# A histogram comparison whose constant operand moves from SBUF to a PSUM bank

## The chip, the cores and the metric

The kernel runs on one NeuronCore of a Trainium2 chip. The core has a matrix engine (PE, TensorE), a vector engine (DVE, VectorE), a scalar engine (ACT, ScalarE), a general engine (POOL, GpSimd) and a queue engine for transfers (SP, SyncE). They run at the same time and are held together by semaphores only. SBUF is the on-chip memory for operands, PSUM the smaller one into which PE writes its sums; DVE and ACT can read and write both. The metric is the time of one execution on the device in microseconds (us), lower is better.

## The reference, cut to what matters

The program is a chain: a convolution block with 32 paths, local attention, and a mixture-of-experts layer whose gate is a graph attention over 262,144 random edges between 16,384 nodes. The part that matters here prepares and runs the graph attention:

```
e      = leaky_relu(a_src[src] + a_dst[dst])
alpha  = softmax of e over the edges with one dst
agg    = segment_sum(h[src] * alpha, dst)        # scores of the experts
hh     = gelu(x @ W1[ei] + b1[ei]); out += g * (hh @ W2[ei] + b2[ei])
```

The kernel sorts the edges by dst in an earlier phase. To know where each node's edges end, it counts the edges of each node (a histogram over 16,384 nodes) and sums the counts up.

## The kernel before, in words

Seven phases follow one another, with a barrier of all engines between them. The change lies in the fifth, `edge_phase` (from L1333), which runs from about 2829 us to 5962 us of the profiled span. Each engine has its own hand-written instruction list there.

**Histogram.** Each dst is split into two digits of 7 bits. For one group of 8 edges per partition, DVE makes two comparison masks ("hot"), one per digit: it compares the constant row 0..127 (`iota`), repeated 8 times, with 8 digits, each repeated 128 times. That is one `tensor_tensor` of 128 partitions x 1024 elements per digit (L1491), f32 in and bf16 out. There are 256 groups, so 512 such instructions; PE multiplies the two masks of a group in 8 matmuls of 128x128 (L1614) that all add into `psC`, which is a part of the PSUM bank `psH[0]`. The masks have two buffers, so DVE is at most two groups ahead of PE. Then DVE turns the counts into positions (L1498 to L1509) and signals `placed`.

**Gathers.** POOL issues one indirect DMA for each of the 16 x 128 columns of edges (L1453): 128 rows of the table `scratch_table`, picked by the edge's src that lies in the SBUF tile `edge[s]`, into `row[s]`. There are AHEAD = 4 buffers, so the first 4 x 128 = 512 gathers wait for nothing but the edges. POOL's list is: `e_zeros` memset, 512 gathers, one gather of first values (L1460), then a wait for the constants, for the zeros in `scratch_b` and for `placed`, then 128 scatters (L1465) that place each node's value at the position of its first edge, a plain DMA (L1470), and then the other 1536 gathers in a loop, each group of 128 after a new load of `edge[s]`.

**Scans.** SP loads `bsrc` from `scratch_b` after all scatters have landed (L1422). DVE then runs the scans over the edges, chunk by chunk (L1529 to L1558), each after the 128 gathers of its chunk; ACT does the exponentials (L1590). SP stores the state and reloads `edge[s]`.

**Experts.** After `placed`, PE, ACT and DVE work through 49 tiles of the expert layer: PE multiplies into `psH[0]` to `psH[3]` (L1626), ACT applies Gelu (L1582), PE multiplies into `psY` (L1631), and DVE adds a bias that lies in SBUF to what it reads from `psY` (L1516). DVE's list takes 3 of these tiles before each scan chunk.

Nothing here is set by a planner; the order on each engine is the order of the code.

Of the kernel before, what the change touches and what calls it, by code (L numbers as in the profile page):

```python
# [12 lines left out]
ACT = mybir.ActivationFunctionType  # L13
# [110 lines left out]
HOT = 8  # L124
# [1208 lines left out]
def edge_phase(nc, io, z_dram, table_dram, adst_dram, digit_dram, edge_dram, node_dram, first_dram, b_dram, state_dram, y_dram):  # L1333
# [6 lines left out]
    with ExitStack() as ctx:  # L1340
        sb = lambda name, shape, dt=F32: ctx.enter_context(nc.sbuf_tensor(name, shape, dt))
        sb2 = lambda name, shape, dt=F32: [sb(f"{name}{i}", shape, dt) for i in range(2)]
        sem = lambda name: ctx.enter_context(nc.semaphore(name))
        sem2 = lambda name: [sem(f"{name}{i}") for i in range(2)]
# [5 lines left out]
        iota = sb("i_iota", [128, 128]); before = sb("i_before", [128, 128])  # L1350
        digit = [sb(f"i_digit{i}", [128, 2, FC]) for i in range(2)]
        hot = [[sb(f"i_hot{i}{d}", [128, HOT, 128], BF16) for d in range(2)] for i in range(2)]
# [18 lines left out]
        psH = [ctx.enter_context(nc.psum_tensor(f"f_psH{e}", [128, ZT], F32)) for e in range(EXPERTS)]  # L1371
        psY = [ctx.enter_context(nc.psum_tensor(f"f_psY{i}", [128, ZT // 128, EXPERTS * C], F32)) for i in range(2)]

        psC, psB = psH[0][:, 0:128], psH[1][:, 0:1]
        passed = sem("passed")
        const_in = sem("const_in"); weights_in = sem("weights_in"); zeroed = sem("zeroed"); b_zeroed = sem("b_zeroed"); b_placed = sem("b_placed")
        b_gathered = sem("b_gathered")
        b_in = sem2("b_in"); state_out = sem2("state_out")
        edge_in = [sem(f"edge_in{i}") for i in range(AHEAD)]; rows_in = [sem(f"rows_in{i}") for i in range(AHEAD)]
        hist_in = sem("hist_in"); zeroed_hot = sem("zeroed_hot"); digit_in = sem2("digit_in")  # L1380
        hot_ready = sem("hot_ready"); hot_used = sem("hot_used"); counted = sem("counted"); step = sem("step")
        totals = sem("totals"); based = sem("based"); placed = sem("placed"); placed_out = sem("placed_out")
        GROUPS = FC // HOT
# [13 lines left out]
        with nc.Block() as block:  # L1397
# [78 lines left out]
            def _(dve):  # L1476
# [5 lines left out]

                dve.memset(zero[:], 0.0).then_inc(zeroed_hot, 1)
                dve.wait_ge(hist_in, 32)
                with dve.Fori(0, NFC // 2) as turn:
                    for par in range(2):
                        dve.wait_ge(digit_in[par], (turn + 1) * 16)
                        for g in range(GROUPS):
                            dve.wait_ge(hot_used, turn * (2 * GROUPS) + par * GROUPS + g)
                            for d in range(2):  # L1490
                                m = dve.tensor_tensor(hot[g % 2][d][:], iota[:].unsqueeze(1).to_broadcast([128, HOT, 128]),  # L1491
                                                      digit[par][:, d, g * HOT:(g + 1) * HOT].unsqueeze(2).to_broadcast([128, HOT, 128]),
                                                      ALU.is_equal)
                            m.then_inc(hot_ready, 1)
# [73 lines left out]

            @block.scalar
            def _(act):  # L1570
                for a, name in ((w1, "ffn_w1"), (b1, "ffn_b1"), (w2, "ffn_w2")):
                    act.dma_start(a[:], io[name]).then_inc(weights_in, 16)
                for par in range(2):
                    act.dma_start(z[par][:], z_view[par]).then_inc(z_in[par], 16)
                act.wait_ge(weights_in, 48)

                def gelus(turn, q, load):

                    t, par = turn * (2 * PER) + q, q % 2
                    for e in range(EXPERTS):  # L1580
                        act.wait_ge(hid_ready, t * EXPERTS + e + 1)
                        act.activation(hid[e][:], psH[e][:], ACT.Gelu, bias=b1[:, e:e + 1]).then_inc(gelu_done, 1)  # L1582
                    if load:
                        act.dma_start(z[par][:], z_view[t + 2]).then_inc(z_in[par], 16)
                    act.wait_ge(y_done[par], turn * PER + q // 2 + 1)
                    act.dma_start(y_view[t], y[par][:]).then_inc(y_out[par], 16)

                def exps(turn, par):
                    act.wait_ge(limited, turn * 2 + par + 1)
                    act.activation(weight[:], drop[:], ACT.Exp).then_inc(exped, 1)  # L1590

                def both(turn, last):
                    for par in range(2):
                        for q in range(par * PER, (par + 1) * PER):
                            gelus(turn, q, not last or q < 2 * PER - 1)
                        exps(turn, par)

                with act.Fori(0, NFC // 2 - 1) as turn:
                    both(turn, False)
                both(NFC // 2 - 1, True)  # L1600
                gelus(NFC // 2, 0, False)
                act.wait_ge(y_out[0], 16 * (TILES_Z // 2 + 1))
                act.wait_ge(y_out[1], 16 * (TILES_Z // 2))
# [414 lines left out]
```

## Time and profile before

| | us |
|---|---|
| median of 3 runs | 6376.89 |
| lowest, highest | 6370.15, 6381.33 |
| profiled execution, its time | 6396.85 |
| profiled execution, its span | 6395.3 |

The span is what the profile covers; 1.55 us of the profiled execution's time lie around it. Busy shares over the whole span are POOL 50%, DVE 50%, PE 48% and ACT 20%, but they are means over phases with different limits: PE and DVE carry the convolution and the attention in the first 2600 us, while POOL is busy for nearly all of the rest. An indirect DMA on POOL shows as busy for as long as POOL works on issuing it; the transfer itself runs later on the DMA engines. In a list of instructions in order of time, "issue" ahead of an instruction is a gap in which the engine waited for nothing that the profile shows.

### The profile page before, as it was taken

Reading aid. Unit: us, or ns where it says so; the run is one execution under the profiler, and the core shown is the slowest. Engines: PE = TensorE matmul, PEld = TensorE weight load, DVE = VectorE, ACT = ScalarE, POOL = GpSimd, SP = SyncE. Lnnn points to the kernel's source line nnn. Section 1 sums busy time; section 2 is a strip of 40 time slices with the busy share of each in tenths; the row PEclk is TensorE's granted clock in tenths of the full one; section 3 lists DMA queues with packets and bytes.
Section 4 is the critical chain, followed back from the end, with each engine's and each line's share of the span. In section 5 each row is a group of like instructions: output and inputs, shape, how many; then the busy total and the mean of one; then the engine's idle time right before and its main releaser. Section 6 shows DMA issues by size and latency. Waiting matters only on the chain. (4 is left out here: it accounts for less than half of the span.)

```text
span 6395.3 us, 60586 instructions
## 1 busy us (share of the span) xinstructions
PE 3078.2 (48%) x16144; PEld 2121.2 (33%) x16144; DVE 3183.0 (50%) x4772; ACT 1270.0 (20%) x4613; POOL 3228.6 (50%) x3313
## 2 busy tenths in 40 slices
PE   2778777775998988454444004822222222222000
PEld 0334434333888887343333002511111111111000
DVE  4989888864877777349994002311110011111139
ACT  0112121112777776210000001200000000000000
POOL 0000000000665655138887776777777777777536
PEclk9788878775999999555555555555555555555555
DMA  6455555553655555330001101311111111111125
GB/s 143 78 84 87 83 83 83 82 79 67 92 88 83 89 84 78 98 87 8 8 9 20 8 4 50 88 31 33 22 27 33 33 33 33 32 32 29 26 74 212
DMA packets 584849, 385.76 MB, mean 60 GB/s; under 512 B 404800, under 2 KB 531552, under 8 KB 581744
## 3 DMA queue, kind: packets, MB, share of 16 engines
q1 hardware_dynamic: 385640, 221.54, 15.4%
q10 hardware_dynamic: 89320, 109.87, 9.4%
q0 software_dynamic: 109728, 52.69, 7.1%
q14 instruction: 120, 0.98, 0.1%
q8 instruction: 41, 0.67, 0.0%
HBM read 235.33 MB, written 147.68 MB: 60 GB/s over the span
## 5 line engine op out<-in xcount | busy, mean ns | idle before, releaser
L1453 POOL DMA_INDIRECT e_row<-scratch_table,e_edge x2048 | 2236.6, 1092 | 704.9 <-issue 674.7
L1631 PE MATMUL f_psY<-f_w,f_hid 128*128 128x64 f32 x1568 | 347.3, 423 | 1839.3 <-ACT f_hid L1582 1839.3
L1631 PEld LDWEIGHTS f_psY<-f_w,f_hid 128*128 128x128 f32 x1568 | 338.1, 332 | 1914.0 <-ACT f_hid L1582 1788.7
L925 POOL MEMSET a_wproj<- 128x128 f32 x1 | 0.2, 204 | 1544.2 <-POOLq L140 1544.2
L1533 DVE TENSOR_TENSOR e_e<-e_row,e_b 128x512 f32<-128x512 f32 x16 | 11.2, 698 | 1324.6 <-DMA e_row<-scratch_table,e_edge 1324.4
L768 DVE SCALAR_TENSOR_TENSOR acc<-psE,c_b,acc 128x448 f32<-128x448 f32 x840 | 568.0, 676 | 107.7 <-PE psE L461 91.2
L1491 DVE TENSOR_TENSOR i_hot<-i_iota,i_digit 128x1024 bf16<-128x1024 f32 x512 | 581.5, 1206 | 9.4 <-DMA i_before<-in_before 9.4
L461 PE MATMUL psE<-stack,c_w 72*128 72x448 bf16 x896 | 386.8, 450 | 335.6 <-DVE acc L768 181.5
L1030 ACT ACTIVATE prob<-psS,low 128x100 f32<-128x100 f32 x1568 | 512.3, 371 | 176.8 <-DVE low L1063 176.8
L448 PE MATMUL psH<-h,c_w 128*128 128x448 f32 x1008 | 525.5, 608 | 0.9 <-ACT h L551 0.9
L1614 PE MATMUL f_psH<-i_hot 128*128 128x128 bf16 x2048 | 264.7, 310 | 326.9 <-DVE i_hot L1491 326.9
L971 PE MATMUL psS<-keys,q_exp 84*128 84x100 f32 x3136 | 394.0, 283 | 53.3 <-DMA keys<-in_kfeat 53.0
L971 PEld LDWEIGHTS psS<-keys,q_exp 84*128 84x128 f32 x3136 | 378.4, 200 | 63.8 <-issue 58.7
L1590 ACT ACTIVATE e_weight<-e_drop 128x1024 f32<-128x1024 f32 x16 | 16.9, 1056 | 1851.9 <-DVE e_drop L1546 1851.9
L1030 ACT ACTIVATION_READ_ACCUMULATOR prob<-psS,low 128x1 f32 x1568 | 367.5, 234 | 0.0
L1626 PE MATMUL f_psH<-f_z,f_w 64*128 64x512 f32 x392 | 352.4, 1077 | 2.3 <-DVE i_posi L1509 2.3
L461 PEld LDWEIGHTS psE<-stack,c_w 72*128 72x128 bf16 x896 | 95.5, 111 | 709.9 <-DVE acc L768 479.0
L1614 PEld LDWEIGHTS f_psH<-i_hot 128*128 128x128 bf16 x2048 | 197.2, 141 | 394.3 <-DVE i_hot L1491 394.3
L945 POOL DMA_DIRECT2D scratch_t<-t x224 | 151.0, 678 | 333.2 <-issue 175.1
L1582 ACT ACTIVATE f_hid<-f_psH,f_b 128x512 f32<-128x512 f32 x196 | 129.4, 687 | 944.9 <-PE f_psH L1626 944.7
L933 POOL DMA_DIRECT2D val<-scratch_vpad x448 | 268.2, 601 | 68.7 <-PE psO L996 33.6
L1063 DVE TENSOR_REDUCE low<-psS 128x5 f32<-128x500 f32 x336 | 216.0, 643 | 149.8 <-PE psS L971 145.8
(273 smaller groups left out, 5401.0 us busy)
## 6 DMA issues: line engine op xcount, KB each, us to landing
stack<-scratch_parts ACTq DMA_DIRECT2D x504, 112.0 KB
e_row<-scratch_table,e_edge POOLq DMA_INDIRECT x2048
scratch_y<-f_y ACTq DMA_DIRECT2D x49, 512.0 KB
g_y<-scratch_y SPq DMA_DIRECT2D x28, 896.0 KB, 4.9
scratch_state<-e_state SPq DMA_DIRECT2D x16, 1536.0 KB, 6.0
val<-scratch_vpad SPq DMA_DIRECT2D x672, 35.0 KB
scratch_parts<-h2p ACTq DMA_DIRECT2D x56, 336.0 KB, 2.2
keys<-scratch_kpad SPq DMA_DIRECT2D x112, 155.0 KB
```

Of the source, the lines that this page charges most:

```text
L448: m = pe.matmul(psH2[:, 0:PIX].rearrange("p (y x) -> p y x", x=W), w2[:, tap, :], h1[:, ROWS * t + dy:ROWS * (t + 1) + dy, dx:dx + W], sta ...
L461: pe.matmul(psE[c % 2][:, 0:PIX], w3[:, c, :], stack[SLOT[t]][:, c, :], start=True, stop=True).then_inc(e_ready, 1)
L768: dve.scalar_tensor_tensor(acc[:, SLOT[t]], psE[c % 2][:, 0:PIX], b3[:, c:c + 1], acc[:, SLOT[t]], ALU.max, ALU.add).then_inc(stt_done, 1)
L933: pool.dma_start(val[st.par][ky * WIN:(ky + 1) * WIN], windows(n, s * QROWS + ky)).then_inc(v_rest[st.at], 16)
L971: m = pe.matmul(psS[bank][:, (blk - a) * KEYS:(blk - a + 1) * KEYS], q_exp[st.pair][:, par, blk].rearrange("k h m -> k (h m)"), keys[par][ ...
L1030: m = act.activation(prob[par][:, blk * KEYS:(blk + 1) * KEYS], psS[bank][:, (blk - a) * KEYS:(blk - a + 1) * KEYS], ACT.Exp, bias=low[par ...
L1063: dve.tensor_reduce(low[par][:, a:b], psS[bank][:, 0:(b - a) * KEYS].rearrange("p (b k) -> p b k", k=KEYS), AX.X, ALU.min)\
L1453: pool.indirect_dma_start(out=row[s][:, f, :], out_offset=None, in_=table_dram, in_offset=bass.IndirectOffsetOnAxis(ap=edge[s][:, 0, f:f + ...
L1491: m = dve.tensor_tensor(hot[g % 2][d][:], iota[:].unsqueeze(1).to_broadcast([128, HOT, 128]), digit[par][:, d, g * HOT:(g + 1) * HOT].unsq ...
L1614: m = pe.matmul(psC, hot[g % 2][1][:, c, :], hot[g % 2][0][:, c, :], start=False, stop=False)
L1626: pe.matmul(psH[e][:], w1[:, e, :], z[par][:], start=True, stop=True).then_inc(hid_ready, 1)
L1631: m = pe.matmul(psY[par][:, j, e * C:(e + 1) * C], hid[e][:, j * 128:(j + 1) * 128], w2[:, e, :], start=True, stop=True)
```

## The change

The kernel takes `psI`, 128 columns of the PSUM bank `psH[2]`, which nobody uses before the expert tiles. At the start of `edge_phase` ACT waits for the loads of `iota` and `before` (`hist_in`), copies `iota` from SBUF into `psI`, and signals `iota_set`; DVE waits for that once, ahead of its histogram loop. In the loop, the first operand of the 512 comparisons is `psI` where it was `iota`. The number of instructions, the shapes, the types and the other operand (`digit`, in SBUF) stay.

```
-        psC, psB = psH[0][:, 0:128], psH[1][:, 0:1]
+        psC, psB, psI = psH[0][:, 0:128], psH[1][:, 0:1], psH[2][:, 0:128]
...
-        hist_in = sem("hist_in"); zeroed_hot = sem("zeroed_hot"); digit_in = sem2("digit_in")
+        hist_in = sem("hist_in"); iota_set = sem("iota_set"); zeroed_hot = sem("zeroed_hot"); digit_in = sem2("digit_in")
...
                 dve.memset(zero[:], 0.0).then_inc(zeroed_hot, 1)
                 dve.wait_ge(hist_in, 32)
+                dve.wait_ge(iota_set, 1)
...
-                                m = dve.tensor_tensor(hot[g % 2][d][:], iota[:].unsqueeze(1).to_broadcast([128, HOT, 128]),
+                                m = dve.tensor_tensor(hot[g % 2][d][:], psI.unsqueeze(1).to_broadcast([128, HOT, 128]),
                                                       digit[par][:, d, g * HOT:(g + 1) * HOT].unsqueeze(2).to_broadcast([128, HOT, 128]),
                                                       ALU.is_equal)
...
             def _(act):
+                act.wait_ge(hist_in, 32)
+                act.activation(psI, iota[:], ACT.Copy).then_inc(iota_set, 1)
                 for a, name in ((w1, "ffn_w1"), (b1, "ffn_b1"), (w2, "ffn_w2")):
                     act.dma_start(a[:], io[name]).then_inc(weights_in, 16)
```

The only list that changes its sequence is ACT's, at the start of the phase. Before, behind the barrier (a row is an instruction's number, its line, its kind and tiles, and what it waits for; a semaphore may stand there under another name, since numbers are used again):

```order
490 L1221 UNCONDITIONAL_BRANCH
491 L1569 UNCONDITIONAL_BRANCH [waits barrier_Pool_Activation_PE_DVE_SP_release]
492 L1572 DMA f_w<-in_ffn_w 64x512
493 L1572 DMA f_b<-in_ffn_b 128x4
494 L1572 DMA f_w<-in_ffn_w 128x256
495 L1574 DMA f_z<-scratch_z 64x512 x2
496 L1598 UNCONDITIONAL_BRANCH [waits weights_in]
```

The same place with the change:

```order
490 L1221 UNCONDITIONAL_BRANCH
491 L1570 UNCONDITIONAL_BRANCH [waits barrier_Pool_Activation_PE_DVE_SP_release]
492 L1573 ACTIVATE f_psH<-i_iota 128x128 [waits hist_in]
493 L1575 DMA f_w<-in_ffn_w 64x512
494 L1575 DMA f_b<-in_ffn_b 128x4
495 L1575 DMA f_w<-in_ffn_w 128x256
496 L1577 DMA f_z<-scratch_z 64x512 x2
497 L1601 UNCONDITIONAL_BRANCH [waits weights_in]
```

The copy now stands ahead of the five loads of the expert layer, which are issued only after it. On DVE, PE, POOL and SP no instruction changes its place.

## Rows read from the trace of the kernel before

**Rows 1.** The page: spans in 40 slices (tenths busy), and POOL's costliest group.

```profile
PE   2778777775998988454444004822222222222000
...
DVE  4989888864877777349994002311110011111139
...
POOL 0000000000665655138887776777777777777536
...
L1453 POOL DMA_INDIRECT e_row<-scratch_table,e_edge x2048 | 2236.6, 1092 | 704.9 <-issue 674.7
```

**Rows 2.** POOL in time, start of the phase: start us, us, engine, line, [idle before].

```profile
2833.75 1.07 POOL L1453 DMA_INDIRECT e_row<-scratch_table,e_edge  x1 [4.12 <-issue]
...
2837.67 0.95 POOL L1453 DMA_INDIRECT e_row<-scratch_table,e_edge  x1 [0.30 <-issue]
...
2840.17 1.96 POOL L1453 DMA_INDIRECT e_row<-scratch_table,e_edge  x1 [0.30 <-issue]
```

**Rows 3.** POOL in time, end of the histogram and end of the first gathers.

```profile
3419.22 1.96 POOL L1453 DMA_INDIRECT e_row<-scratch_table,e_edge  x1 [0.30 <-issue]
3421.49 0.94 POOL L1453 DMA_INDIRECT e_row<-scratch_table,e_edge  x1 [0.31 <-issue]
...
3743.25 0.94 POOL L1460 DMA_INDIRECT e_b_first<-scratch_adst,e_first_ix  x1 [0.30 <-issue]
3744.50 1.03 POOL L1465 DMA_INDIRECT scratch_b<-e_node_dst,i_posi  x1 [0.30 <-issue]
```

**Rows 4.** L1453 alone in two stretches: us, POOL busy (count), clock, DMA share, GB/s.

```profile
2840.00:3421.00 581.00, 497.77 (x254) 0.50 0.08 14
3430.00:3740.00 310.00, 229.84 (x245) 0.50 0.12 15
```

**Rows 5.** DVE in time: the histogram's first merged row, and the last positions.

```profile
2838.91 61.44 DVE L1491 TENSOR_TENSOR i_hot<-i_iota,i_digit 128x1024 bf16<-128x1024 f32 x54 [9.43 <-DMA i_before<-in_before]
...
3424.86 0.30 DVE L1509 CAST i_posi<-i_pos 128x256 int32<-128x256 f32 x1
```

**Rows 6.** DVE's groups by shape: count, busy us, mean ns, idle before.

```profile
L1491 DVE TENSOR_TENSOR i_hot<-i_iota,i_digit 128x1024 bf16<-128x1024 f32 x512 | 581.5, 1206 | 9.4 <-DMA i_before<-in_before 9.4
...
L1073 DVE TENSOR_TENSOR prob<-prob,inv 128x1400 f32<-128x1400 f32 x112 | 181.1, 1617 | 3.9
...
L1085 DVE TENSOR_TENSOR own<-own 128x448 f32<-128x448 f32 x112 | 70.0, 625 | 3.9
...
L1516 DVE TENSOR_TENSOR f_y<-f_psY,f_b 128x1024 f32<-128x1024 f32 x49 | 59.6, 1216 | 417.8 <-PE f_psY L1631 417.8
...
L208 DVE COPY sort_key<-psTurn 128x512 f32<-128x512 f32 x28 | 28.2, 1009 | 1.4 <-PE psTurn L240 1.3
...
L1529 DVE TENSOR_TENSOR_SCAN e_b<-e_edge,e_b,e_bsrc 128x128 f32<-128x128 f32 x64 | 25.7, 465 | 448.4 <-DMA e_bsrc<-scratch_b 448.4
```

**Rows 7.** POOL and DVE in time, scan phase.

```profile
3963.44 1.22 DVE L1516 TENSOR_TENSOR f_y<-f_psY,f_b 128x1024 f32<-128x1024 f32 x1 [12.82 <-PE f_psY L1631]
3964.59 1.60 DVE L1529 TENSOR_TENSOR_SCAN e_b<-e_edge,e_b,e_bsrc 128x128 f32<-128x128 f32 x4
...
3974.16 2.26 DVE L1552 TENSOR_TENSOR e_part<-e_row,e_weight 128x2048 f32<-128x2048 f32 x1
...
3963.89 0.94 POOL L1453 DMA_INDIRECT e_row<-scratch_table,e_edge  x1 [0.30 <-issue]
...
3974.28 2.97 POOL L1453 DMA_INDIRECT e_row<-scratch_table,e_edge  x1 [0.30 <-issue]
...
3978.79 1.19 POOL L1453 DMA_INDIRECT e_row<-scratch_table,e_edge  x1 [0.30 <-issue]
```

**Rows 8.** DVE in time, convolution phase.

```profile
300.06 0.67 DVE L768 SCALAR_TENSOR_TENSOR acc<-psE,c_b,acc 128x448 f32<-128x448 f32 x1
300.66 1.21 DVE L202 TENSOR_TENSOR sort_key<-sort_other 128x1024 f32<-128x1024 f32 x1
301.79 0.67 DVE L768 SCALAR_TENSOR_TENSOR acc<-psE,c_b,acc 128x448 f32<-128x448 f32 x1
```

**Rows 9.** POOL in time: a pause, the scatters' end, the loop's first and last gather.

```profile
3892.65 0.98 POOL L1465 DMA_INDIRECT scratch_b<-e_node_dst,i_posi  x1 [2.96 <-issue]
...
3913.06 0.62 POOL L1470 DMA_DIRECT2D scratch_b<-e_b_first  x1 [1.41 <-DMA scratch_b<-e_node_dst,i_posi]
3943.86 0.99 POOL L1453 DMA_INDIRECT e_row<-scratch_table,e_edge  x1 [30.18 <-DMA e_edge<-scratch_edge]
...
5940.90 0.94 POOL L1453 DMA_INDIRECT e_row<-scratch_table,e_edge  x1 [0.30 <-issue]
```

**Rows 10.** DVE's group L1533; waits of PE and SP (us in total, times, longest).

```profile
L1533 DVE TENSOR_TENSOR e_e<-e_row,e_b 128x512 f32<-128x512 f32 x16 | 11.2, 698 | 1324.6 <-DMA e_row<-scratch_table,e_edge 1324.4
...
PE f_psH L1614 <- DVE i_hot L1491: 326.9, 256, 11.5
...
SPq L1418 <- DVE i_posi L1509: 76.8, 1, 76.8
```

**Rows 11.** ACT in time: its last small copy, the old position of the loads.

```profile
2826.33 0.29 ACT L1327 ACTIVATE t_rows<-t_psR 128x140 f32<-128x140 f32 x1 [3.27 <-PE t_psR L1309]
...
2829.10 0.56 ACTq L1572 DMA_DIRECT2D f_w<-in_ffn_w  x1
```

## What it does to the time: the prediction

> **What bounds the kernel now.** I read the page's slices first: from slice 27 on only POOL is busy, at 7 tenths or so, with PE at 2 and DVE at 0 to 1 [rows 1]. So the busy shares of the whole span say nothing of this phase; the question is who ends last in it. The waits answer: DVE waits 1324.6 us for the gathered rows in its 16 chunks [rows 10], and POOL's gathers wait for almost nothing but their own issue: 704.9 us over 2048 of them, 674.7 of it the usual gap [rows 1]. POOL's list is therefore the chain through the whole of the edge phase: 512 gathers, one more, 128 scatters, 1536 gathers.
>
> Then POOL in order of time. The first gathers take 0.95 us with a gap of 0.30 [rows 2]. From 2840.17 on they take 1.96, until 3419.22; the next, at 3421.49, takes 0.94 again [rows 2, 3]. Those two instants are the start and the end of DVE's 512 comparisons, which begin at 2838.91 [rows 5] and run without a gap (581.5 us busy in all [rows 6]). The two stretches by themselves: 254 gathers in the first with 497.77 us busy, mean 1.96; 245 in the second with 229.84, mean 0.94 [rows 4]. Something that DVE does in the histogram doubles the cost of a gather.
>
> What it is, the scan phase shows, where single DVE instructions meet gathers. A gather that starts at 3974.28, just inside a tensor_tensor with both inputs in SBUF (3974.16, 2.26 us long), takes 2.97 us: it ends 0.83 us after that instruction. A gather beside the scans, two SBUF inputs again but short ones, takes 1.19. But the gather at 3963.89 lies wholly inside an L1516 (3963.44, 1.22 us long), which adds an SBUF bias to a PSUM operand, and takes 0.94, as if alone [rows 7]. So a gather is held until the running DVE instruction ends if that has two SBUF inputs, and not if one of them is in PSUM. In the histogram the held gather plus its gap of 0.30 take 1.96 + 0.30 = 2.26 us, two DVE instructions (61.44 us for 54 in a merged row is 1.138 each [rows 5]).
>
> After the histogram POOL still has 252 gathers and the L1460 to go: DVE signals at 3425.2 [rows 5], POOL reaches the scatters at 3744.50 [rows 3]. For 319 us the positions lie ready. The histogram's own length is hidden; its effect on POOL is not.
>
> **The change part by part.**
>
> *The gathers.* The new comparison has the form of L1516: PSUM first, SBUF second, 128x1024. By rows 7 it holds no gather. Per gather the histogram stretch costs now: 3421.49 - 2840.17 = 581.32 us over 254 gathers = 2.289; the free stretch 3743.25 - 3421.49 = 321.76 us over 253 issues = 1.272 [rows 2 to 4]. Both contain the same kind of pauses, about 3 us once in 128 issues (one is visible at 3892.65 [rows 9]), two in each stretch, so they cancel. Gain: 254 x (2.289 - 1.272) = **258.3 us**. Bounds: below, if a gather stayed as slow as beside the scans, 1.19 + 0.30 = 1.49 in place of 1.25 [rows 7], the gain would be 258.3 - 254 x 0.24 = 197 us; above, nothing can make it faster than the free gather, 258 (a few us more if the unprofiled gather is shorter).
>
> The Trainium skill has two things on this (SBUF — State Buffer, section "Who interferes with whom"): a vector instruction with two SBUF inputs contends with a GpSimd instruction that reads SBUF, one with a single SBUF input does not. By that the sum is as above. But the same section argues, as an inference, that tensor_tensor does not stall a DMA's issue on GpSimd, because it takes only the read interface and writing descriptors needs the write interface; by that rule there would be no loss to take away and the time would stay at 6377. The trace disagrees with that inference: 1.96 against 0.94 us.
>
> *The comparison itself.* Reading PSUM may cost DVE more. Instruction to instruction, the SBUF comparison takes 1.13 to 1.14 us, and an element costs (1617 - 625) / (1400 - 448) = 1.042 ns by L1073 and L1085 [rows 6], 1.067 us for 1024; a sort comparison of the same size, both inputs in SBUF, starts its successor after 1.13 (300.66 to 301.79 [rows 8]). Beside it the L768, with PSUM in and 448 elements, starts its successor after 0.60 [rows 8]; 448/1024 of the element time is 0.467, so it has 0.13 us around its elements where the SBUF one has 0.065. That is +0.07 us an instruction. The nearest in shape, L1516, starts its successor after 1.15 (3963.44 to 3964.59 [rows 7]), +0.015; its mean length is 1216 against 1206 ns [rows 6]. So between 512 x 0.015 = 8 us and 512 x 0.07 = 36 us more histogram; I take 30, near the upper one, since the L768 rows stand among back-to-back work. A gain is excluded, the element rate being the same. The signal `placed` moves from 3425.2 to about 3456, at most 3461.
>
> The Trainium skill (Perfetto Trace Analysis, section "Optimizing Scalar/DVE Operations") gives about 60 ns of access overhead on SBUF and 125 ns on PSUM for DVE; by that it would be 512 x 0.065 = 33 us, and the rows of L768 agree with it (0.065 and 0.13).
>
> *What hides it.* POOL now reaches the scatters at 3744.5 - 258.3 = 3486.2. DVE's 3456 is 30 us earlier. The cover shrinks from 319 us to 30, but holds: it is gone when a comparison costs more than (3486.2 - 3425.2) / 512 = 0.12 us extra, a pitch above 1.255. From there on, each 0.01 us costs 5 us.
>
> *The copy on ACT.* One 128x128 activation, in the place of one like L1327 (0.29 us [rows 11]); DVE's start moves by 0.3 to 0.6 us, inside the cover, cost 0. Had it been on the chain, it would be that. Queued behind ACT's new wait are its five loads, so far issued from 2829.10 [rows 11], now from about 2839. Whoever needs them is PE, which waits for `placed` as well, 600 us later: cost 0. PE in the histogram waits 326.9 us for DVE [rows 10], so it has room at any rate. SP's store of positions (L1418) and the three expert tiles ahead of the first scan come 30 us later; DVE then idles 448.4 us before the first scan [rows 6], now about 448 - 258 - 30 = 160. Cost 0.
>
> *Behind it.* From L1465 on all is as before, shifted: scatters, L1470, SP's load, one chunk, `edge` reload, gather loop (3943.86 becomes 3686) [rows 9]. The loop stays POOL's; nothing in it reads the moved operand. No stall there goes, none comes.
>
> **Sum.** Span 6395.3 - 258.3 = 6137.0; the profiled time, 6396.85, becomes 6138.6. The median of the runs shown is 20 us below the profiled time (6376.89), so the prediction is 6376.89 - 258.3 = 6118.6, rounded **6119 us**, 4.05% less.
>
> **The rivals.**
>
> *A, the hold stays.* The second input may come through the contended path whatever the first is, or it is the bf16 output (L1516 writes f32) that holds. Then a gather still takes two comparisons. With comparisons 0.07 us longer and 254 gathers (two in each): +254 x 0.14 = +36 us, 6413, slower by 0.6%; with 0.015 longer +8, 6385. It decides as soon as the hold exists at all. For it: only a bf16 output differs from L1516. Against: the gather inside L1516 at 0.94, and L1552 with f32 output holding for 2.97 [rows 7], so the output's type is not what holds there. 5%.
>
> *B, half a hold.* Gathers at 1.49 as beside the scans: 6377 - 197 = 6180. For it: nothing with one SBUF input shows it. 3%.
>
> *C, DVE becomes the bound.* The repeated reads of the same 128 PSUM columns could be slow. From a pitch of 1.255 the gain shrinks: at 1.40 `placed` comes at 3425 + 512 x 0.263 = 3560, 74 us after POOL, and the time is 6193. It turns slower than before when the pitch passes 1.135 + 319/512 = 1.76 us. At the rate of the slowest DVE read of PSUM here, L208 with 1009 ns for 512 elements [rows 6], it would be 2.02 us, `placed` at 3425 + 453 = 3878, and the time 6377 + 134 = 6511. For it: L208. Against: L1516 has PSUM, a repeated operand and the same size at 1216 ns. 3% for the range between, 1% for slower.
>
> **How the numbers follow.** Forecast 88%, A 5%, B 3%, C 4%. The forecast's own range: the pauses may fall otherwise (3 us each, two of them), chance meetings of gathers and DVE in the loop of 1536 may differ by 10 us, the runs lie within 11 us of each other, and up to 6 us if DVE's pitch just passes 1.255: 6095 to 6145. B and C's near end are just outside; I set 6095 to 6150, which leaves out about 15%. A difference of 0.2%, 13 us, is what a measurement can tell from none. Faster: 0.88 + 0.03 + 0.03 = 0.94; same: A's low end, 0.02; slower: A's high end and C's far end, 0.04.
>
> **What would show each step.** The 254 gathers between 2840 and 3421 become some 460 in the same time, at 0.94 to 0.96 us; if they stay at 1.9 to 2.1, A holds; at 1.2, B. The group of L1492 shows the comparison's cost: 512 instructions in 590 to 617 us of busy time. L1460 stands near 3485 and the first scatter right behind it without a wait; a wait for DVE's `i_posi` there would be C. The last gather of the phase moves from 5940.90 [rows 9] by the same 258 us. The prediction is wrong if the gathers shorten and the end doesn't follow, which would need a chain that no row here shows.

## The result and the profile after

The changed kernel takes **6116.49 us** (median of 4 runs, 6115.78 to 6125.72) against 6373.52 us of the kernel before on the same chip (6369.09 to 6381.33): a ratio of 0.9594 [0.9575, 0.9613], 4.1% faster. The forecast was 6119. The profiled execution takes 6116.39 us, its span 6114.8.

First the page: slices, and the two groups that the change touches (the first answers to [rows 1], the second to [rows 6]).

```profile
DVE  4998888985587778536999214111111111100139
...
POOL 0000000000466556325777757777777777777536
...
L1453 POOL DMA_INDIRECT e_row<-scratch_table,e_edge x2048 | 1975.1, 964 | 704.1 <-issue 673.8
...
L1492 DVE TENSOR_TENSOR i_hot<-f_psH,i_digit 128x1024 bf16<-128x1024 f32 x512 | 579.3, 1208 | 7.6 <-ACT f_psH L1573 7.6
```

The gathers' busy time falls from 2236.6 to 1975.1 us and their idle time stays: 261.5 us less, where the medians differ by 257.0. While DVE is at 9, POOL now shows 7 tenths, as in the scan phase, where it showed 8 before, part of it time in which gathers were held. The comparison has not become dearer at all, 1208 ns against 1206.

POOL in order of time, from the phase's start to the end of the scatters, the loop's first gather, and one of its last (answers to [rows 2, 3, 9]).

```profile
2809.98 0.53 POOL L1446 MEMSET e_zeros<- 128x512 f32 x1 [8.38 <-POOLq L1221]
2813.89 1.07 POOL L1453 DMA_INDIRECT e_row<-scratch_table,e_edge  x1 [3.38 <-issue]
...
2822.80 0.94 POOL L1453 DMA_INDIRECT e_row<-scratch_table,e_edge  x1 [0.30 <-issue]
...
3464.85 0.94 POOL L1460 DMA_INDIRECT e_b_first<-scratch_adst,e_first_ix  x1 [0.30 <-issue]
3466.10 1.03 POOL L1465 DMA_INDIRECT scratch_b<-e_node_dst,i_posi  x1 [0.30 <-issue]
...
3634.67 0.62 POOL L1470 DMA_DIRECT2D scratch_b<-e_b_first  x1 [1.42 <-DMA scratch_b<-e_node_dst,i_posi]
3665.56 0.99 POOL L1453 DMA_INDIRECT e_row<-scratch_table,e_edge  x1 [30.27 <-DMA e_edge<-scratch_edge]
...
5659.54 0.94 POOL L1453 DMA_INDIRECT e_row<-scratch_table,e_edge  x1 [0.30 <-issue]
```

From the first gather to L1460 it is 3464.85 - 2813.89 = 650.96 us; before it was 3743.25 - 2833.75 = 909.50 [rows 2, 3]. The difference is 258.5 us. The scatters follow without a wait, and the stretch from L1460 to the loop's first gather is 200.7 us as before (3943.86 less 3743.25 is 200.6). The last gather moves by 281 us, not by 258, because in this execution the whole phase begins earlier (the first gather at 2813.89 instead of 2833.75, 19.9 us), and the loop of 1536 gathers is 3 us shorter (1994.0 against 1997.0). The 19.9 us belong to earlier stages that the change does not touch: the profiled execution of before lay 20 us above its median. The medians differ by 257.0.

L1453 alone in two stretches, during the histogram and after it (answers to [rows 4]; us, POOL busy and count, clock, DMA share, GB/s).

```profile
2820.00:3399.00 579.00, 430.94 (x458) 0.50 0.13 18
3405.00:3455.00 50.00, 35.53 (x39) 0.50 0.20 48
```

458 gathers in the histogram where 254 were, at a mean of 0.94 us in place of 1.96, the same as once DVE is done.

DVE's first merged row and its last positions (answers to [rows 5]).

```profile
2817.99 12.53 DVE L1492 TENSOR_TENSOR i_hot<-f_psH,i_digit 128x1024 bf16<-128x1024 f32 x11 [7.63 <-ACT f_psH L1573]
...
3401.77 0.29 DVE L1510 CAST i_posi<-i_pos 128x256 int32<-128x256 f32 x1
```

Instruction to instruction that is (12.53 - 1.21) / 10 = 1.132 us; the SBUF form, by the same working, had (61.44 - 1.21) / 53 = 1.136. The positions are ready at 3402, 63 us before POOL reaches L1460.

ACT in order of time: its copy, and the loads behind it (answers to [rows 11]).

```profile
2817.32 0.28 ACT L1573 ACTIVATE f_psH<-i_iota 128x128 f32<-128x128 f32 x1 [9.74 <-DMA i_before<-in_before]
2817.32 0.56 ACTq L1575 DMA_DIRECT2D f_w<-in_ffn_w  x1
```

The waits: in total, times, longest (answers to [rows 6, 10]).

```profile
DVE e_e L1534 <- DMA e_row<-scratch_table,e_edge: 1321.1, 12, 119.7
...
PE f_psH L1617 <- DVE i_hot L1492: 322.9, 256, 9.7
DVE e_b L1530 <- DMA e_bsrc<-scratch_b: 193.2, 1, 193.2
```

DVE's waits for rows are unchanged: the loop of 1536 gathers is still POOL's. Only the idle time ahead of the first scan shrinks, from 448.4 to 193.2 us.

### The profile page after: what moved, and what is told of

It is laid out like the page before. It is cut to its first block and busy times, and to the rows that moved or that the text cites. A ratio compares the mean times of both kernels' runs of the same rounds, so it can differ in the third digit from the quotient of the medians.

```text
span 6114.8 us, 60588 instructions
## 1 busy us (share of the span) xinstructions
PE 3076.0 (50%) x16144; PEld 2113.0 (35%) x16144; DVE 3180.6 (52%) x4772; ACT 1269.8 (21%) x4614; POOL 2967.1 (49%) x3313
## 5 line engine op out<-in xcount | busy, mean ns | idle before, releaser
L1453 POOL DMA_INDIRECT e_row<-scratch_table,e_edge x2048 | 1975.1, 964 | 704.1 <-issue 673.8
L1534 DVE TENSOR_TENSOR e_e<-e_row,e_b 128x512 f32<-128x512 f32 x16 | 11.2, 699 | 1321.4 <-DMA e_row<-scratch_table,e_edge 1321.1
L768 DVE SCALAR_TENSOR_TENSOR acc<-psE,c_b,acc 128x448 f32<-128x448 f32 x840 | 568.6, 677 | 110.8 <-PE psE L461 94.6
L1492 DVE TENSOR_TENSOR i_hot<-f_psH,i_digit 128x1024 bf16<-128x1024 f32 x512 | 579.3, 1208 | 7.6 <-ACT f_psH L1573 7.6
L933 POOL DMA_DIRECT2D val<-scratch_vpad x448 | 268.3, 601 | 68.7 <-PE psO L996 34.9
## 6 DMA issues: line engine op xcount, KB each, us to landing
stack<-scratch_parts ACTq DMA_DIRECT2D x504, 112.0 KB
```

The source lines that it names most:

```text
L768: dve.scalar_tensor_tensor(acc[:, SLOT[t]], psE[c % 2][:, 0:PIX], b3[:, c:c + 1], acc[:, SLOT[t]], ALU.max, ALU.add).then_inc(stt_done, 1)
L933: pool.dma_start(val[st.par][ky * WIN:(ky + 1) * WIN], windows(n, s * QROWS + ky)).then_inc(v_rest[st.at], 16)
L1453: pool.indirect_dma_start(out=row[s][:, f, :], out_offset=None, in_=table_dram, in_offset=bass.IndirectOffsetOnAxis(ap=edge[s][:, 0, f:f + ...
L1492: m = dve.tensor_tensor(hot[g % 2][d][:], psI.unsqueeze(1).to_broadcast([128, HOT, 128]), digit[par][:, d, g * HOT:(g + 1) * HOT].unsqueez ...
```

## The experiments

Twelve kernels were run, later and on five chips. On all five the kernel before takes 6829 to 6840 us (medians), not 6374, and each ratio below is against its runs on the same chip. Which chip the comparison above ran on is not known, so the 460 us may lie in the chip or in its condition at the time ("condition" below means this difference, whatever its cause); they turned out to matter for the change itself. None of the 460 us lies ahead of the edge phase: its first gather starts at 2813 us in e1, at 2814 in the changed kernel of the comparison.

**The theory** was that a gather is held to the end of the DVE instruction that runs when it starts, if both inputs of that instruction are in SBUF. The rivals were that something else in the change gives the gain (the order of ACT's loads), that the hold is a share of the time rather than an instruction, and that the place of the operand decides.

### e1: all of the change but the operand

```diff
-    m = dve.tensor_tensor(hot[g % 2][d][:], psI.unsqueeze(1)...
+    m = dve.tensor_tensor(hot[g % 2][d][:], iota[:].unsqueeze(1)...
```

> ACT still fills the PSUM columns and DVE still waits for it once, but the 512 comparisons read iota from SBUF as before. Theory (the gain is that a gather is not held by a comparison with two SBUF inputs): nothing is gained, 6373 us within 10, gathers in the histogram at 1.96 us. Rival (the gain comes from the start of the phase: ACT's five loads now stand behind the copy): a time near 6116.

Measured: 6832.85 us, ratio 1.0006 [0.9991, 1.0020]. The copy, the wait and the later loads are worth nothing. POOL of this kernel:

```profile
3000.99 1.98 POOL L1453 DMA_INDIRECT e_row<-scratch_table,e_edge  x1 [0.30 <-issue]
```

A gather in the histogram takes 1.96 us again, and from the first gather to L1460 it is 3728.20 - 2812.91 = 915.3 us.

### e2: SBUF for the first digit, PSUM for the second

```diff
+    m = dve.tensor_tensor(hot[g % 2][d][:], (iota[:], psI)[d].unsqueeze(1)...
```

> Only the second comparison of each pair reads PSUM; the first has both inputs in SBUF again. Theory, a held gather is let go when the running comparison ends: it then takes 0.83 to 0.9 us, the gap is 0.30, so the next gather wants the inputs some 1.2 us later, just after the PSUM comparison of 1.13 us, and meets the next SBUF comparison. It stays in step, one gather in 2.26 us, and the whole gain is lost: 6373 us within 12. Rival, the loss goes with the share of comparisons that hold: half of it, 6116 + 129 = 6245.

Measured: 6826.12 us, ratio 0.9989 [0.9975, 1.0003]. Half of the comparisons no longer hold, and nothing is gained. DVE and then POOL of this kernel, in order of time:

```profile
3000.26 1.21 DVE L1492 TENSOR_TENSOR i_hot<-i_iota,i_digit 128x1024 bf16<-128x1024 f32 x1
3001.39 1.21 DVE L1492 TENSOR_TENSOR i_hot<-f_psH,i_digit 128x1024 bf16<-128x1024 f32 x1
3002.52 1.21 DVE L1492 TENSOR_TENSOR i_hot<-i_iota,i_digit 128x1024 bf16<-128x1024 f32 x1
```

```profile
3000.33 1.97 POOL L1453 DMA_INDIRECT e_row<-scratch_table,e_edge  x1 [0.30 <-issue]
3002.60 1.95 POOL L1453 DMA_INDIRECT e_row<-scratch_table,e_edge  x1 [0.30 <-issue]
```

Each gather starts 0.07 to 0.08 us after an SBUF comparison has begun, is held for the rest of it, ends 0.83 us after it (3002.30 against 3001.47) beside the PSUM one, and after the gap of 0.30 meets the next SBUF one. A held gather with its gap and two comparisons are equally long, 2.27 us, and lock together. The same 0.82 to 0.83 us stand between the comparison's end and the gather's in 253 gathers of the histogram of before. So the hold goes by the instruction; a share of the time would have given half the gain.

### e3: SBUF and PSUM by turns, two comparisons each

```diff
+    m = dve.tensor_tensor(hot[g % 2][d][:], (iota[:], psI)[g % 2].unsqueeze(1)...
```

> Both comparisons of every second group of 8 edges have two SBUF inputs, the other groups read PSUM. The same number of holding comparisons as with one in each pair. Theory: a gather let go at the end of the first SBUF comparison misses the second (it is not asking for anything until 1.2 us later), so the next two run free and the one after is held: 3 gathers in two groups, 4.53 us, 1.51 each, 384 in the histogram in place of 464. Loss 80 x 1.25 = 100 us: 6216 within 15. Rival by share: 6245. Rival that any such comparison in the stretch keeps all gathers in step: 6373.

Measured: 6661.42 us, ratio 0.9735 [0.9705, 0.9765]; one run of the four, left out of the ratio, took 7124.19, as long as e4 below. Why is not known. DVE, then POOL:

```profile
3006.63 2.34 DVE L1492 TENSOR_TENSOR i_hot<-i_iota,i_digit 128x1024 bf16<-128x1024 f32 x2
3008.90 2.34 DVE L1492 TENSOR_TENSOR i_hot<-f_psH,i_digit 128x1024 bf16<-128x1024 f32 x2
3011.16 2.34 DVE L1492 TENSOR_TENSOR i_hot<-i_iota,i_digit 128x1024 bf16<-128x1024 f32 x2
```

```profile
3006.93 1.74 POOL L1453 DMA_INDIRECT e_row<-scratch_table,e_edge  x1 [0.30 <-issue]
3008.97 0.94 POOL L1453 DMA_INDIRECT e_row<-scratch_table,e_edge  x1 [0.30 <-issue]
3010.22 0.94 POOL L1453 DMA_INDIRECT e_row<-scratch_table,e_edge  x1 [0.30 <-issue]
```

Three gathers in 4.53 us, one of them held. The one at 3006.93 ends at 3008.67, 0.83 after its first comparison is over (3006.63 + 1.21 = 3007.84), although the second SBUF one is running by then: of the comparisons only the one that it meets at its start holds it. From the first gather to L1460 it is 3576.91 - 2826.12 = 750.8 us, 164.5 less than in e1. The lock theory gave 158, a share of the time 129.

### e4: the operands exchanged

```diff
-    psI.unsqueeze(1)..., digit[par][:, d, ...]..., ALU.is_equal)
+    digit[par][:, d, ...]..., psI.unsqueeze(1)..., ALU.is_equal)
```

> The digits in SBUF are the first operand and the PSUM columns the second. Theory (the number of SBUF inputs decides): 6116 us within 5, gathers 0.94. Rival (it is the place of the operand: the first operand from SBUF is what holds, or the second from PSUM costs more): gathers at 1.96 and 6373.

Measured: 7123.34 us, ratio 1.0429 [1.0405, 1.0454]: slower by 4.3%, which neither theory had. The gathers were not held, 0.94 to 0.95 us up to about 3050 us, so the operand's place does not decide the hold. From there on many take 1.09 us, 17 of them 1.79, most with no comparison running: the mean of the 512 is 1.02. And DVE stood still for 637.9 us in the histogram. Was that the exchange, or where it ran?

### e9: the changed kernel itself, once more

No edit.

> The changed kernel itself, once more. On the two chips of the experiments so far the kernel before takes 6829 and 6840 us where it took 6374 on the chip of the comparison, and kernels that differ from the changed one only in an operand's place or in 24 gathers take 7123 and 7141. Theory (what differs is the chip or its host, where the other engines are slowed while POOL issues gathers at full rate): if the kernel before takes some 6830 here too, the changed one takes about 7120 to 7140, 4% more, with DVE idle for 20 us at a time in the histogram; if the kernel before takes some 6374, it takes 6116. Rival (it is the swapped operands or the moved gathers that cost): 6116/6374 of the kernel before, 4% less, on any chip.

Measured: 7135.42 us, ratio **1.0433 [1.0410, 1.0455]**. It is not the exchange. The same program that was 4.1% faster in the comparison is 4.3% slower here. DVE in order of time: as the stall builds up, in it, and where it ends.

```profile
2814.18 5.74 DVE L1492 TENSOR_TENSOR i_hot<-f_psH,i_digit 128x1024 bf16<-128x1024 f32 x5
2824.98 2.36 DVE L1492 TENSOR_TENSOR i_hot<-f_psH,i_digit 128x1024 bf16<-128x1024 f32 x2 [5.05 <-remote]
...
2864.22 2.36 DVE L1492 TENSOR_TENSOR i_hot<-f_psH,i_digit 128x1024 bf16<-128x1024 f32 x2 [20.04 <-remote]
...
2998.62 2.36 DVE L1492 TENSOR_TENSOR i_hot<-f_psH,i_digit 128x1024 bf16<-128x1024 f32 x2 [20.04 <-remote]
3021.02 2.36 DVE L1492 TENSOR_TENSOR i_hot<-f_psH,i_digit 128x1024 bf16<-128x1024 f32 x2 [20.04 <-remote]
...
3527.15 73.62 DVE L1492 TENSOR_TENSOR i_hot<-f_psH,i_digit 128x1024 bf16<-128x1024 f32 x65 [12.34 <-remote]
```

And POOL, at the first gathers' end and after it:

```profile
3500.45 0.94 POOL L1460 DMA_INDIRECT e_b_first<-scratch_adst,e_first_ix  x1 [0.30 <-issue]
...
4032.99 1.03 POOL L1465 DMA_INDIRECT scratch_b<-e_node_dst,i_posi  x1 [531.60 <-DVE i_posi L1510]
```

While gathers run free, a group of two comparisons comes once in 22.40 us instead of once in 2.27. The stall builds up over the first groups and ends right after POOL's last gather (L1460 at 3500.45), from where DVE runs unbroken. So only 34 of the 256 groups are done when POOL is finished, and the rest follow at full pace: POOL waits 531.6 us for the positions. The stretch from the first gather to L1460 is 3500.45 - 2808.95 = 691.5 us, 223.8 less than in e1 and 40.5 more than in the comparison. So the change still gains 223.8 us on the gathers and loses 531.6 to the wait, 308 us on balance, beside 302.6 between the medians of e9 and e1. This is rival C of the prediction, DVE as the bound, by a cause that it did not name.

A group has 8 matmuls with 8 weight loads on PE, and 22.40 / 16 = 1.40. In the scan phase DVE waits for PE's expert tiles, of 40 matmuls and 40 weight loads each. In the comparison two of them follow each other in 13.4 to 14.2 us where nothing else stands between; in e9, while POOL issues gathers, in 112.2, and 80 x 1.40 = 112.0:

```profile
4420.30 1.22 DVE L1517 TENSOR_TENSOR f_y<-f_psY,f_b 128x1024 f32<-128x1024 f32 x1 [89.89 <-issue]
4532.46 1.22 DVE L1517 TENSOR_TENSOR f_y<-f_psY,f_b 128x1024 f32<-128x1024 f32 x1 [110.93 <-DMA scratch_vpad<-v]
```

On DVE itself the last 3 of the 16 scans of one chunk stand at the same interval, where nothing is waited for (two of them here); the 13 before them took 5.05 us together:

```profile
4723.95 0.54 DVE L1559 TENSOR_TENSOR_SCAN e_state<-e_weight,e_state,e_part 128x128 f32<-128x128 f32 x1 [1.53 <-issue]
4725.35 0.54 DVE L1559 TENSOR_TENSOR_SCAN e_state<-e_weight,e_state,e_part 128x128 f32<-128x128 f32 x1 [0.87 <-issue]
```

**The second theory**: in this condition, while POOL issues gathers once in 1.25 us, each other engine gets one instruction through in 1.40 us. That also fits the 460 us by which the kernel *before* is slower here. In e1, which takes as long, POOL waits 300.2 us in 6 places for the reload of `edge`, in the comparison 30 us in one place: 270 us. Another 168 lie behind the last gather (6829.7 - 6207.6 = 622.1 us to the end of the span, 454.4 before), since DVE, held up by the expert tiles, ends its scans 187 us after that gather in e1 and some 18 in the comparison.

One thing speaks against taking "one instruction in 1.40 us" word for word. PE in the stall:

```profile
3001.04 1.03 PE L1617 MATMUL f_psH<-i_hot 128*128 128x128 bf16 x8 [21.37 <-DVE i_hot L1492]
```

The 8 matmuls of a group stand 0.11 us apart, right behind DVE's signal, and end by 3002.07 (matmul ends are modelled), yet DVE goes on at 3021.02. So 1.40 is what the total comes to for each of PE's instructions; what passes in the 19 us between is not in the trace.

### e11: eight more matmuls of zeros in each group

```diff
+    pe.matmul(psC, zero[:], zero[:], start=False, stop=False)
```

> The changed kernel with 8 more matmuls in each group on PE (zeros times zeros, added to the same sum). On the slowed chips a group of 8 edges takes 22.40 us while gathers run free, with 2, 3 and 8 DVE instructions in a group alike. Theory (each instruction of PE, 8 weight loads and 8 matmuls in a group, costs 1.40 us there): 32 of them, a group in 44.8 us. Rival (the period comes from the signals between the engines, one pair a group): 22.4 us still. On a chip that is not slowed: 2.27 us, PE's 16 matmuls hidden behind DVE, and 6116.

Measured: 7180.85 us (one run). DVE:

```profile
3002.13 2.35 DVE L1492 TENSOR_TENSOR i_hot<-f_psH,i_digit 128x1024 bf16<-128x1024 f32 x2 [42.45 <-remote]
3046.93 2.35 DVE L1492 TENSOR_TENSOR i_hot<-f_psH,i_digit 128x1024 bf16<-128x1024 f32 x2 [42.45 <-remote]
```

The interval doubles to 44.80 us = 32 x 1.40 when PE's instructions in a group double and DVE's and the signals stay. So it goes by the number of PE's instructions, and the rival is refuted; how each comes to cost 1.40 us is not shown.

### e5, e6, e7: more on DVE

In e5 the kernel before compares in four pieces of 256 elements; in e6 the changed kernel compares a third time in each group, to no use; in e7 it copies 1024 f32 elements in SBUF once in a group.

```diff
+    for u in range(4):                       # e5, with iota in SBUF
+        m = dve.tensor_tensor(hot[g % 2][d][:, u * 2:(u + 1) * 2, :], iota[:]...
-    for d in range(2):                       # e6
+    for d in (2, 0, 1):
+    dve.tensor_copy(copy_out[g % 2][:], copy_in[:])   # e7
```

> The kernel before the change (both inputs in SBUF, no PSUM copy), but each comparison is cut into 4 of 256 elements: 2048 instructions of about 0.27 + 0.065 = 0.33 us, 680 us of histogram in place of 580. Theory (held until the running instruction ends, no longer): a gather that wants its inputs 1.2 to 1.3 us after it was let go is held to the next end of a 0.33 us instruction, about 1.33 us a gather; POOL reaches the scatters after some 512 x 1.33 + 12 = 693 us, DVE is done at about the same time, and the time is 6116 + 40 = 6156 within 20. Rival (the inputs are short for as long as DVE reads two tensors, whatever the length of one instruction): gathers still at 1.96, the histogram 100 us longer, some 6411.

> The changed kernel with a third comparison of the same form in each group (its result is written to a tile that nobody reads): 256 x 1.131 = 290 us more histogram. Theory (POOL's list was the end, with DVE's signal 64 us ahead of it in the profile): the gathers stay at 0.94, POOL waits for the positions 290 - 64 = 226 us, 6116 + 226 = 6342 within 8. Rival (DVE's length is hidden however long): 6116. Rival (DVE was already the end): 6406.

> The changed kernel with one f32 copy of 1024 elements from SBUF to SBUF ahead of each pair of comparisons (source and targets are tiles that nothing else uses). It has one SBUF input, but may read and write through two ports. About 0.6 us each: the histogram is 154 us longer, the end 90 us later by DVE alone, 6206. Rule that a single input never holds: all gathers in the stretch at 0.94. Rule that a copy in a two-port mode holds: a gather that asks during a copy waits for its end, so part of the gathers take up to 0.94 + 0.6 = 1.5 us and the mean rises to about 1.0 to 1.1.

Measured: e5 7227.85 us, ratio 1.0572 [1.0551, 1.0593]; e6 7381.03, 1.0800 [1.0782, 1.0819]; e7 7276.74 (one run). All three fall into the stall of e9, with the same interval of 22.40 us whatever DVE has to do in a group. As times they answer nothing of what they were made for. Three readings remain. The first two are of single gathers: the mean of e5 between 2840 and 3400 (418 gathers at 1.00 us) says nothing, since e9, which has nothing to hold a gather, has 417 at 1.02 there.

In e5, ahead of the stall, 24 pieces with both inputs in SBUF run unbroken, one in 0.34 us:

```profile
2820.47 8.13 DVE L1493 TENSOR_TENSOR i_hot<-i_iota,i_digit 128x256 bf16<-128x256 f32 x24 [9.02 <-DMA i_before<-in_before]
2824.36 1.04 POOL L1453 DMA_INDIRECT e_row<-scratch_table,e_edge  x1 [0.30 <-issue]
```

The gathers beside them take 1.03 to 1.12 us and come once in some 1.34, the 1.33 of the theory: shorter instructions hold for less. In e7 the copy, with one input in SBUF, holds too:

```profile
3021.19 0.69 DVE L1494 COPY copy_out<-copy_in 128x1024 f32<-128x1024 f32 x1 [19.44 <-remote]
3021.26 1.44 POOL L1454 DMA_INDIRECT e_row<-scratch_table,e_edge  x1 [0.30 <-issue]
```

The gather ends at 3022.70, 0.82 us after the copy, as behind a comparison with two SBUF inputs. A gather that had been under way for 0.4 to 0.5 us when the copy began is held as well: those at 2833.47, 2836.24 and 2839.09 take 1.21 to 1.31 us and end 0.12 after the copy. So of the two rules of e7's forecast the second holds. In e6 the time is 246 us above e9, and POOL's wait for the positions 782.0 - 531.6 = 250 us longer, so in that condition the histogram is the bound.

### e8: 24 gathers kept back until after the scatters

```diff
-    for s in range(AHEAD):
+    for s in range(AHEAD - 1):
         gather(0, s)
+    gather(0, AHEAD - 1, 0, FC - 24)
...
+    gather(0, AHEAD - 1, FC - 24, FC)
```

> The changed kernel with POOL's list in another order: the last 24 of the first 512 gathers are issued after the scatters and the plain DMA behind them, where POOL idles 30.3 us for the reload of the edges. Theory (POOL's list is the chain, so what fills its idle time is a gain): the scatters start 30 us earlier, after 488 gathers and still some 30 us after the positions are ready, the idle time is filled, and the time is 6116 - 30 = 6086 within 5. Rival (what is late there is not POOL, or the first scans now wait for the kept gathers): 6116.

Measured: 7141.13 us, ratio 1.0452 [1.0432, 1.0472], beside e9's 1.0433. It was meant to spend the 63 us by which the positions are early; here they are 535.1 us late, so the forecast was not tested in the condition that it was made for. That stays open.

### e10 and e12: gathers a little further apart

If it is the pace of the gathers that decides, a slower POOL makes the kernel faster. Behind each gather POOL writes zeros, to no use: 1 column in e10, 320 in e12, there with the next gather waiting for them.

```diff
     m = pool.indirect_dma_start(...)
+    wait(pool, paced, ...); pool.sem_inc(passed, 1)
+    pool.memset(pad[:], 0.0).then_inc(paced, 1)
```

> The changed kernel with a small memset on POOL (128x1, a tile that nobody reads) behind each of the 2048 gathers, so that a gather comes every 1.45 to 1.6 us and not every 1.25. Theory for the chips on which the kernel before takes some 6835 us: the other engines are slowed only when gathers come faster than about one in 1.4 us (they are not in e3_alternate's histogram, one gather in 1.51 us, and are at one in 1.25), so DVE no longer idles 20 us at a time, the histogram takes 580 us, the scan phase follows POOL, and the time is 6116 + 2048 x 0.25 = 6630 within 150, below the kernel before (6835) and the changed one (7135). Rival (the slowing comes with POOL being busy at all, or with what the unheld gather does to the memory, whatever the pace): DVE still idles 20 us at a time, and the time is 7135 or more. On a chip where the kernel before takes 6374, it is 6630 as well, that is slower.

> The changed kernel with a memset of 128x320 on POOL behind each of the 2048 gathers. The 128x1 memset of e10_paced took 0.12 us and vanished in the gap of 0.30 us between gathers, so the pace stayed one in 1.25; this one should take some 0.37 us (by the 0.20 of 128x128 and the 0.53 of 128x512) and give one gather in 1.5 us, at which e3_alternate's histogram was not slowed. Theory (the pace decides): no 20 us idle times of DVE, histogram 580 us, scans right behind the gathers, 6116 + 2048 x 0.25 = 6630 within 60, against 6835 for the kernel before where it is slowed. Rival (in e3_alternate it was the holding comparisons, not the pace, that kept the others free): DVE still idles about 20 us at a time, 7300 or more.

Measured: e10 6793.29 us, ratio 0.9945 [0.9926, 0.9963]; e12 **6608.87 us, ratio 0.9666 [0.9647, 0.9686]**. e12 came as forecast (6630 within 60); e10 met neither its theory (6630 within 150) nor its rival (7135 or more).

In e10 the memset of 0.12 us mostly vanishes in the gap: the median from gather to gather is still 1.25 us. But 23% of the steps in the histogram are longer, mostly 1.4 to 2.1 us, so the mean is 723.5 / 512 = 1.41, beside 691.5 / 512 = 1.35 in e9 (e12's forecast took it that the pace had stayed). The stall is milder, not gone. DVE stands for 499.9 us in 54 pieces, and an expert tile takes some 54 to 57 us, about half of e9's 112.2, up to the last gathers:

```profile
5894.46 1.23 DVE L1521 TENSOR_TENSOR f_y<-f_psY,f_b 128x1024 f32<-128x1024 f32 x1 [55.62 <-DMA scratch_vpad<-v]
5948.49 1.23 DVE L1521 TENSOR_TENSOR f_y<-f_psY,f_b 128x1024 f32<-128x1024 f32 x1 [52.80 <-DMA scratch_vpad<-v]
```

e12, POOL in time and DVE's group:

```profile
3000.33 0.95 POOL L1454 DMA_INDIRECT e_row<-scratch_table,e_edge  x1 [0.16 <-POOL pad L1459]
3001.28 0.38 POOL L1459 MEMSET pad<- 128x320 f32 x1
3001.83 0.95 POOL L1454 DMA_INDIRECT e_row<-scratch_table,e_edge  x1 [0.17 <-POOL pad L1459]
```

```profile
L1496 DVE TENSOR_TENSOR i_hot<-f_psH,i_digit 128x1024 bf16<-128x1024 f32 x512 | 579.3, 1210 | 7.4 <-DMA i_before<-in_before 7.4
```

With 1.50 us from gather to gather no stall is left: DVE idles 7.4 us where e9 had 639.4, and 2048 gathers that each cost 0.25 us more make a kernel that is some 526 us faster than e9 (on another chip, so read it by the ratios: 0.9666 against 1.0433). Spacing the gathers takes the stall away, and e10, between the two in both pace and stall, fits a pace that decides. But one thing is left: in e12 POOL also waits for a signal ahead of each gather, in e10 it does not, and no run has the one without the other. Under the condition of the experiments e12 is the best version; where free gathers disturb nobody, as in the comparison, 2048 x 0.25 = 512 us more POOL should make it slower than 6116. It was not run in that condition.

## Why the prediction was right

*What bounds the phase.* POOL's list, and behind the histogram nothing else: right. L1465 waits for nothing, and DVE's wait for rows stays (1321.1 us).

*The gathers.* The term was 254 x (2.289 - 1.272) = 258.3 us; the stretch from the first gather to L1460 lost 258.5. e1 shows that the operand alone does it, e2 and e3 that the mechanism is the one read from [rows 7]: held to the end of the running instruction. What the prediction did not see is what follows for partial cures: 1.96 us is no fixed price but a lock of two periods. That the sum came within 3 us of the median (6119 against 6116.49) is also because the forecast took the whole gain and nothing off it, and nothing came off.

The Trainium skill (SBUF — State Buffer, section "Who interferes with whom") has it that a vector instruction with at most one SBUF input, outside the 2-port modes of DVE, does not contend with GpSimd: for the comparison the trace agrees, 0.94 to 0.96 us in all 458. Its inference that tensor_tensor leaves the issue of a DMA on GpSimd alone does not hold for these indirect DMAs: 1.96 us in e1 against 0.94 in the changed kernel. For plain DMAs it does. In the attention phase of the changed kernel POOL issues them beside L1073, whose two inputs lie in SBUF:

```profile
1594.48 1.17 POOL L933 DMA_DIRECT2D val<-scratch_vpad  x2
1594.78 1.62 DVE L1073 TENSOR_TENSOR prob<-prob,inv 128x1400 f32<-128x1400 f32 x1
```

The second of the two starts inside L1073 and is over by 1595.65, 0.75 us ahead of L1073's end; all 197 of L933 that meet an L1073 take 0.59 to 0.64 us, and with nothing running the median is 0.59. So what is held here is the indirect issue, which takes its row numbers from the SBUF tile `edge[s]`; that it is the reading of them that waits is argued, not shown.

*The comparison.* Mis-sized: 30 us more was forecast, and it is 2 us less (579.3 against 581.5 busy). L1516 was the nearer row in shape and gave 8; L768 has another operation and other work around it, and its 0.13 us did not carry over to this instruction. The Trainium skill's 125 against 60 ns (Perfetto Trace Analysis, section "Optimizing Scalar/DVE Operations") does not show in these 512 back-to-back instructions, whatever it is in single ones. The error cost nothing, since the cover held: 63 us instead of 30.

*The copy on ACT.* 0.28 us as forecast, and not on POOL's chain. That ACT's loads now stand behind it even let DVE start a little earlier: 8.0 us after L1446, 9.8 before. e1, with the same loads and the SBUF operand, has 7.9.

*The idle time before the first scan.* 193 us against 160 forecast: the same mis-sized 30 us.

*What it left out.* The prediction took it that a freed gather costs the other engines nothing, and had only one trace for it. In the comparison it holds. In the condition of the experiments the same freed gathers stall the histogram for as long as they last, and the change costs 4.3%. No row of the trace of before could have shown it: there DVE and PE run at full pace beside gathers at one in 1.25 us in the scan phase too. Its 0.04 for slower speaks of that condition alone.

## What to carry to other kernels

Here a vector instruction with two inputs in SBUF holds the indirect DMA issue of GpSimd that starts while it runs (a plain DMA it does not), and an SBUF to SBUF copy does so with one input (e7). One broadcast constant moved to PSUM frees them, and the comparison costs no more for it. Whether the kernel gets faster is another question: 4.1% in one condition, 4.3% slower in the other. Two loops that hold each other may be locked in step: half the cure then gives nothing when it comes every other instruction (e2), and 64% of the whole when it comes in pairs (e3: 164.5 of 258.5 us). When an engine is freed, ask what its faster pace does to everybody else, and time it more than once and on more than one chip.

## What the hardware showed that was not expected

On the five chips of the experiments, indirect DMAs issued once in 1.25 us cut PE to about one instruction in 1.40 us on the mean (22.40 us for 16 instructions, 44.80 for 32, 112.2 for 80), and three DVE scans of 0.54 us also come once in 1.40. At a mean of 1.41 (e10, beside 1.35 in e9's histogram) it is about half as bad. At one gather in 1.50 (e12) nothing is slowed, nor is the histogram at 1.51 on the mean (e3's profiled run) or 2.27 (e1, e2); one run of e3 took 7124.19, and what it did is not on record. POOL is not spared either: in e4 and e9 part of its own gathers come once in 1.40 from about 3050 us on. The Trainium skill says in the section named above that PE and ACT never wait on anyone; of their SBUF ports that may hold, but no run here bears it out for their pace. What is shared and why the comparison was spared was not settled; that it is the supply of instructions to the engines is only argued from the price per instruction, and the burst of 8 matmuls in 1.03 us shows that a supply, if it is one, is not even. The scatters were not slow to land in either case (L1470 waits 1.4 us for all 128), which speaks against a backlog of the DMA queue.
